# A transformer stack on one core: gate moved into the output projection's weights, residual added from PSUM, new instruction orders

## The reference

```
x = x + gate1 * (self_attention(modulate(ln(x))) @ W_o + b_o)     # gate1: one value per feature
x = x + cross_attention(ln(x) or x, context) @ W_oc + b_oc
x = x + gate2 * (gelu(modulate(ln(x)) @ W1 + b1) @ W2 + b2)
```

## Time and profile before

| | us |
|---|---|
| median of 3 runs | 2904.0 (2903.85 to 2904.89) |
| profiled execution | 2907.48 |
| its span, first to last instruction | 2905.7 |
| PE busy | 2775.7 (96%) |
| DVE busy | 1765.5 (61%) |
| ACT busy | 1542.6 (53%) |
| POOL busy | 699.1 (24%) |
| mean granted clock of PE | 0.975 |

### The profile page before, as it was taken

The page is one execution under the profiler, slowest core; times in us unless marked ns, Lnnn a source line. Parts: engine busy times, 40 slices in busy tenths (PEclk is TensorE's granted clock), DMA queues, the critical chain, the costliest instruction groups (busy, mean ns, idle before and its releaser), DMA issues. The chain is left out here.

```text
span 2905.7 us, 61884 instructions
## 1 busy us (share of the span) xinstructions
PE 2775.7 (96%) x23508; PEld 2275.6 (78%) x23508; DVE 1765.5 (61%) x3583; ACT 1542.6 (53%) x2707; POOL 699.1 (24%) x760
## 2 busy tenths in 40 slices
PE   7999999995899999999999999999999999999998
PEld 6999999994677777777777777777777777777866
DVE  2444444435576776776766767667666666666652
ACT  3444444432455555655556555655565556556653
POOL 3333343321122221222212212212122121121111
PEclk8999999996799999999999999999999999999998
DMA  5122222104335444445454443543545435445421
GB/s 160 44 78 80 69 69 69 40 8 134 95 79 114 100 104 109 102 106 124 100 143 97 101 107 95 120 105 92 130 103 136 102 90 112 99 94 109 103 66 36
DMA packets 276950, 277.90 MB, mean 96 GB/s; under 512 B 90352, under 2 KB 206432, under 8 KB 276656
## 3 DMA queue, kind: packets, MB, share of 16 engines
q1 hardware_dynamic: 264752, 251.26, 36.0%
q10 hardware_dynamic: 11904, 22.68, 2.3%
HBM read 99.03 MB, written 29.56 MB: 44 GB/s over the span
## 5 line engine op out<-in xcount | busy, mean ns | idle before, releaser
L1957 ACT ACTIVATE p_f<-score 128x1024 f32<-128x1024 f32 (+1 forms) x576 | 560.8, 1019 | 319.4 <-PE obank L3095 138.5
L2459 DVE TENSOR_REDUCE m_a<-score 128x4 f32<-128x1024 f32 x384 | 458.3, 1217 | 48.2 <-PE score L3061 48.1
L3165 PE MATMUL gbank<-w,h_c 128*128 128x256 f32 x1536 | 396.0, 392 | 1.9 <-ACT h_c L1974 1.9
L3165 PEld LDWEIGHTS gbank<-w,h_c 128*128 128x128 f32 x1536 | 274.6, 190 | 48.1 <-ACT h_c L1974 2.3
L1146 PE MATMUL m_ps<-m_comb,m_w 128*128 128x256 f32 x2304 | 295.4, 284 | 1.5 <-PEq L253 1.5
L1146 PEld LDWEIGHTS m_ps<-m_comb,m_w 128*128 128x128 f32 x2304 | 279.9, 188 | 5.0 <-issue 3.6
L819 ACT ACTIVATE m_hf<-m_ps,tab 128x256 f32<-128x256 f32 x192 | 80.5, 470 | 246.9 <-PE m_ps L1146 246.9
L1781 POOL TENSOR_TENSOR res_a<-res_a,bias_a 128x512 f32<-128x512 f32 x48 | 64.2, 1336 | 577.3 <-DMA bias_a<-rows_L 577.3
L3095 PE MATMUL obank<-p_f,v_s 128*20 128x256 f32 x3072 | 200.8, 391 | 1.1 <-ACT p_f L1957 0.8
L761 POOL TENSOR_TENSOR m_hhl<-m_hf,m_hhl 128x512 fp32r<-128x512 f32 x96 | 125.2, 1304 | 318.8 <-DVE m_hhl L985 318.8
L1789 POOL TENSOR_TENSOR c_rstd<-c_mv,eps 128x2 f32<-128x2 f32 x48 | 9.3, 194 | 742.3 <-DVE c_mv L2412 742.3
(11 more groups left out here) (282 smaller groups left out, 5572.6 us busy)
## 6 DMA issues: line engine op xcount, KB each, us to landing
k_cat<-k_hl SPq DMA_DIRECT2D x288, 128.0 KB, 3.6
q_cat<-q_hl SPq DMA_DIRECT2D x288, 128.0 KB, 4.1
qc_cat<-qc_hl SPq DMA_DIRECT2D x288, 128.0 KB, 3.2
split_L<-m_cut SPq DMA_DIRECT2D x24, 512.0 KB, 5.8
x_a<-x_after_L SPq DMA_DIRECT2D x48, 256.0 KB, 4.0
res_a<-x_after_L SPq DMA_DIRECT2D x48, 256.0 KB, 2.8
kc_cat<-kc_hl SPq DMA_DIRECT2D x288, 39.0 KB, 1.9
x_after_L<-y_c SPq DMA_DIRECT2D x32, 256.0 KB, 3.2
```

The lines of the kernel that those rows point to most:

```text
L1957: e.activation(p_f[i % 4][0:n, :], score[i % 2].ap[0:n, :, :].rearrange("p h n -> p (h n)"), ACT.Exp, scale=SCALE).then_inc(ex.sem, 1)
L2459: e.tensor_reduce(m_a[:, :, i::NPAIR].rearrange("p t h -> p h t"), score[i % 2].ap[:, :, :].rearrange("p h (t k) -> p h t k", t=TT), AX.X, ...
L3165: mm = e.matmul(B_DOWN.ap[:, tt, :], h_c[:, k, tt * P:(tt + 1) * P], weights_of(d)["w2"][:, k, :], start=(k == 0), stop=(k == MC - 1))
```

## The change

The self projection multiplies by weights whose columns already carry the gate: POOL makes them per unit (`self_out_gated`), one unit ahead. The input is loaded straight into x_b, POOL adds the bias row there, and DVE adds the projection out of PSUM. res_a is gone. The loads of the input now wait for cross_residual and cross_turned of the unit before.

```
-        x_a, res_a = tile("x_a"), tile("res_a")
+        x_a = tile("x_a")
+        o_gated = sb("o_gated", [P, CC, D])
 load_residual(a):                                            # SP
-                    e.wait_ge(*S["T_xb"].at(a - 1))
-                x_load(a, res_a, S["A_x"])
+                    e.wait_ge(*S["K_res"].at(a - 1))
+                    e.wait_ge(*S["K_xt"].at(a - 1))
+                x_load(a, x_b, S["A_x"])
 self_residual(a):                                            # POOL
-                    bias_added(res_a, res_a, bias_a[:, :], S["A_res"])
-            def self_sum(a):
-                    e.wait_ge(*S["T_y"].at(a))
-                    e.wait_ge(*S["A_res"].at(a))
-                    e.tensor_tensor(x_b[:, :, :], x_b[:, :, :], res_a[:, :, :], ALU.add).then_inc(S["T_xb"].sem, 1)
+                    bias_added(x_b, x_b, bias_a[:, :], S["A_res"])
+            def self_out_gated(a):                            # POOL
+                e.wait_ge(*S["A_gate"].at(a))
+                if a:
+                    e.wait_ge(*S["T_op"].at(a - 1))
+                if a % NB == 0:
+                    e.wait_ge(*W_in["o"].at(a // NB))
+                e.tensor_tensor(o_gated[:, :, :], W["o"][:, :, :], gate_a[:, :].unsqueeze(1).to_broadcast([P, CC, D]),
+                                ALU.mult).then_inc(S["T_og"].sem, 1)
-            def self_gated(a):                                # DVE
-                e.wait_ge(*S["A_gate"].at(a))
-                    e.wait_ge(*S["K_res"].at(a - 1))
-                    e.wait_ge(*S["K_xt"].at(a - 1))
-                e.tensor_tensor(x_b[:, :, :], B_T.ap[:, :, :], gate_a[:, :].unsqueeze(1).to_broadcast([P, TT, D]),
-                                ALU.mult).then_inc(S["T_y"].sem, 1)
+            def self_sum(a):                                  # DVE
+                e.wait_ge(*S["T_op"].at(a))
+                e.wait_ge(*S["A_res"].at(a))
+                e.tensor_tensor(x_b[:, :, :], B_T.ap[:, :, :], x_b[:, :, :], ALU.add).then_inc(S["T_xb"].sem, 1)
 self_projected(a):                                           # PE
-                weights_in(a, "o")
-                turn(B_T, S["T_y"], a)
-                by_token(B_T, 0, oT_a, W["o"])
+                e.wait_ge(*S["T_og"].at(a))
+                turn(B_T, S["T_xb"], a)
+                by_token(B_T, 0, oT_a, o_gated)
```

The written-out orders of all engines are new, in the loop as well as in the opening and the drain. PE's loop (+ the beginning of one iteration after, - before):

```
+ self_plain(m, 4); cross_values(b, 2); cross_values(b, 3); up(c, 1); self_plain(m, 5); self_plain(m, 6);
+ self_recips_spread(a); cross_keys_values(a); self_projected(a); up(c, 2); self_plain(m, 7); self_turned(q);
+ up(c, 3); self_max_rows(m); cross_turned(a); keys(q); cross_queries(a); cross_recips_spread(b); queries(q);
+ self_scores(n - 2, 0); self_scores(n - 2, 1); cross_projected(b); down(n - 5, 0..3); self_values(n - 2, 0); ...
- cross_keys_values(n - 4); self_turned(n - 2); self_max_rows(n - 3); cross_turned(n - 4); up(n - 6, 3);
- cross_queries(n - 4); keys(n - 2); queries(n - 2); self_scores(a, 0..1); cross_recips_spread(n - 5); down(d, 0..1);
- self_scores(a, 2..3); cross_projected(n - 5); down(d, 2); ... up(c, 0); up(c, 1); self_recips_spread(a);
- self_plain(m, 4..5); cross_values(b, 3); self_projected(a); context_turned(a); self_plain(m, 6..7); up(c, 2)
```

POOL's loop, before and after:

```
- context_rstd(n - 2); cross_residual(a); self_residual(n - 2); mlp_sum(n - 5); self_rstd(n); mlp_residual(n - 4);
- self_sum(n - 2); cross_rstd(n - 2); mlp_rstd(n - 3)
+ context_rstd(n - 2); mlp_rstd(n - 4); self_rstd(n); mlp_sum(n - 5); self_residual(n - 2); self_out_gated(n - 1);
+ mlp_residual(n - 4); cross_rstd(n - 2); cross_residual(n - 2)
```

```
-            e.wait_ge(*S["store"].at(NB - 1))
+            e.wait_ge(*S["store"].at(NB - 2))
+            e.wait_ge(s_last, 16)                              # DVE, blocks
+            e.memset(k_cat[0][:, :, :].bitcast(F32), -1.0).then_inc(s_ones, 1)
```

```
-            e.wait_ge(s_first, 64)
+            e.wait_ge(s_qk, 1)
+            e.tensor_copy(mix["wqk"][:, :, :], ps_qk[:, :, :]).then_inc(s_done, 1)
+            e.wait_ge(*S["xt"].at(0))
+            e.wait_ge(s_first, 48)
```

More of the change, by code:

```diff
@@ L3429, in _ @@
             self_plain(3, 4)
+            cross_values(1, 3)
             up(0, 1)
+            self_plain(3, 5)
             self_recips_spread(2)
-            self_plain(3, 5)
             self_plain(3, 6)
-            cross_values(1, 3)
+            cross_keys_values(2)
             self_projected(2)
+            up(0, 2)
             self_plain(3, 7)
-            up(0, 2)
+            self_turned(4)
+            up(0, 3)
+            self_max_rows(3)
+            cross_turned(2)
+            keys(4)
+            cross_queries(2)
+            queries(4)
+            cross_recips_spread(1)
+            self_scores(3, 0)
+            self_scores(3, 1)
+            down(0, 0)
+            down(0, 1)
+            down(0, 2)
+            cross_projected(1)
+            self_scores(3, 2)
+            self_scores(3, 3)
+            down(0, 3)
+            self_values(3, 0)
+            cross_plain(2, 0, 0)
+            cross_plain(2, 0, 1)
+            self_scores(3, 4)
+            self_values(3, 1)
+            cross_plain(2, 1, 0)
+            cross_plain(2, 1, 1)
+            down(0, 4)
+            self_scores(3, 5)
+            cross_plain(2, 2, 0)
+            self_scores(3, 6)
+            cross_plain(2, 2, 1)
+            down(0, 5)
+            cross_plain(2, 3, 0)
+            self_scores(3, 7)
+            cross_plain(2, 3, 1)
+            down(0, 6)
+            cross_max_rows(2)
+            down(0, 7)
+            self_plain(4, 0)
+            self_plain(4, 1)
+            self_values(3, 2)
+            mlp_turned(1)
+            self_values(3, 3)
+            cross_scores(2, 0)
+            cross_scores(2, 1)
+            values(4, 0)
+            values(4, 1)
+            cross_scores(2, 2)
+            cross_values(2, 0)
+            cross_values(2, 1)
+            context_turned(3)
+            cross_scores(2, 3)
+            self_plain(4, 2)
+            up(1, 0)
+            self_plain(4, 3)
             for n in range(6, 47):
@@ L3441, in _ @@
                     e.wait_ge(s_w[layer(n)], 16 * n_w[layer(n)])
-                cross_keys_values(n - 4)
-                self_turned(n - 2)
-                self_max_rows(n - 3)
-                cross_turned(n - 4)
-                up(n - 6, 3)
-                cross_queries(n - 4)
-                keys(n - 2)
-                queries(n - 2)
-                self_scores(a, 0)
-                self_scores(a, 1)
-                cross_recips_spread(n - 5)
-                down(d, 0)
-                down(d, 1)
@@ L3545, in _ @@
-            self_values(44, 3)
-            self_plain(45, 1)
-            cross_scores(43, 0)
-            mlp_turned(42)
-            values(45, 0)
-            cross_scores(43, 1)
-            cross_scores(43, 2)
-            values(45, 1)
-            context_turned(44)
-            cross_scores(43, 3)
-            cross_values(43, 0)
-            cross_values(43, 1)
+                self_turned(q)
+                up(c, 3)
+                self_max_rows(m)
+                cross_turned(a)
@@ new lines, in _ @@
+                cross_plain(n - 3, 3, 1)
+                down(n - 5, 6)
+                cross_max_rows(n - 3)
+                down(n - 5, 7)
+                self_plain(n - 1, 0)
+                self_plain(n - 1, 1)
+                self_values(n - 2, 2)
+                self_values(n - 2, 3)
+                mlp_turned(n - 4)
+                values(n - 1, 0)
+                cross_scores(n - 3, 0)
+                cross_scores(n - 3, 1)
+                values(n - 1, 1)
+                context_turned(n - 2)
@@ L3633, in _ @@
             up(43, 2)
+            cross_keys_values(45)
+            self_turned(47)
+            self_max_rows(46)
             self_projected(45)
-            self_turned(47)
             up(43, 3)
-            self_max_rows(46)
             cross_turned(45)
```

1143 lines of the change are left out of this document (550 added, 593 removed).

## The result

The kernel after takes 2891.8 us (median of 4, 2887.7 to 2895.8), the kernel before in the same session 2904.4 us. The ratio is 0.9943, 95% interval 0.9929 to 0.9958: faster by 0.57%, which is 16.5 us (the two medians lie 12.7 us apart), beyond the 0.2% that can be told from nothing. The direction was forecast, the 44 us were not: about a third of them came, and 2891.8 lies at the edge of the stated range of 2826 to 2892.

What follows compares the result with a forecast made beforehand. PE bounds the steady loop (busy 1790 of 1838 us). Terms of 16, 8, 5.3, 10, 2.4 and 2 sum to 44 us off the profiled 2907.5, giving 2863.5, or 2860 for the runs' median; range 2826 to 2892.

Steps and rivals of the forecast that it cites:

- x_a's wait less gelu's: Steady loop: 1.15 us of wait removed before cross_turned, 0.75 added before self_turned; 0.40 net per iteration, 16 us.
- The border: Before the blocks: no wait for the last store, and k_cat fills moved off self_normed(0); 5.3 us won.
- The preparation: Before the border: router rows and context copy come earlier, the gain capped by the anchor loads; 2.4 us won.
- Rival C: SyncE's load_residual waits for cross_residual and holds up the max rows: 82 us lost in the loop, 2942 us; chance 0.08.
- The other edges in the loop: Steady loop: SyncE's and ScalarE's orders, the gate's row and the residual landing in x_b cost nothing, hidden by PE's work.
- rival B: The removed wait returns whole at self_turned and cross_turned, GpSimd's chain having 0.3 us to spare: 2876 or 2884 us; chance 0.20.
- The loop: The 41 steady iterations: 16 us from the exchanged waits and 8 us from the joints.
- the joints: Steady loop: down(d, 0..3) made contiguous wins 0.2 us per iteration, 8 us.
- Filling: From 669.5 to 819.5 us: self_turned(2), values(1) and queries put in gaps win 10 us.
- Rival D: The order does as forecast, but preparation and filling give nothing: 2872 us; chance 0.12.
- The drain: Final stretch of 248.5 us: one GpSimd link less per unit wins 2 us, bounds -3 and 6.
- rival A: Steady loop: no gelu stall, or a faster chain after it, so the whole 1.15 us goes: 2829 us; chance 0.15.

Runs made afterwards that it cites:

- e3_gate_only: Kernel before with only the gate moved onto the projection's weights and the residual added from PSUM, orders otherwise kept: ratio 0.9992 to the kernel before.
- e6_normed_later: Kernel after with VectorE's self_normed(n) moved behind self_max(n-1, 0) and (n-1, 1): ratio 0.9895 to the kernel before.
- e1_border: Kernel before with only the new preparation and border; loops, filling and drain in the old orders: ratio 0.9984 to the kernel before.
- e13b_filling: Kernel after with context_stats(0) and context_normed(0) behind keys_low(0) and ScalarE's five weight loads issued first: ratio 0.9933 to the kernel before.
- e2: Kernel before with only up(c, 3) moved ahead of self_max_rows and cross_turned in the loop: ratio 1.0259, 75 us slower.
- e7: Kernel after with ScalarE's five weight loads issued at the start of the blocks: ratio 0.9945 to the kernel before.
- e8: Kernel after with VectorE's context_stats(0) and context_normed(0) moved behind keys_low(0): ratio 0.9940 to the kernel before.
- e10: Kernel of e6_normed_later with ScalarE's next_queries_keys also moved behind cross_weights(n-3, 0): ratio 0.9882 to the kernel before.
- e11: Kernel after with the sixteen matmuls of down(0..3) cut again into 8, 4 and 4: ratio 1.0013 to the kernel before.
- e12b_bank_again: Kernel after with self_turned writing bank g1 instead of g0, run again for its profile: 2895.7 us in one execution.
- e9_three: Kernel after with self_turned on g1, self_normed behind two self_max, and mlp_residual behind cross_rstd and held until xT_b is made: 2850.7 us, ratio 0.9806.
- e5_bank_pool: Kernel after with self_turned on g1 and GpSimd's cross_rstd ahead of mlp_residual: ratio 0.9961 to the kernel before.

## Why the prediction was right in direction and wrong in size

**What held.** The bound, PE's stalls of one place in the loop. The wait for x_a went. The new stall before self_turned: forecast 0.70 as idle time, "in its place 41 waits of about 0.7 us"; it is 41 of 0.59. Of the loop's terms x_a's wait less gelu's: forecast 0.40 net, measured 0.98 - 0.59 = 0.39, 16 us in 41 periods. The border: forecast 5.3; x_a's first turn is 7.5 us earlier and the mixture's last group 2.1 (645.52 against 647.65), which leaves 5.3. (By the earlier trace rows the prediction had the normalising end 0.8 us past the fills. It ends at 669.41, 1.0 us past the two of k_cat, and behind them came a third fill, of kc_cat, which ended at 668.95.) The preparation: 2.4 forecast, 2.2 measured (the mixture begins at 59.51, before at 61.69). The gate on the projection: nil, and e3_gate_only shows it. Rival C did not come: 3.5 us of waits for max rows, and their cause is the weights in ScalarE's queue, not load_residual in SyncE's.

**The failed steps.**

1. "The other edges in the loop ... I cost at nothing: PE's work hides them." The list named SyncE's and ScalarE's orders and left VectorE's out. There self_normed(n) was put between mlp_gated and self_max(n-1, 0), just when GpSimd starts mlp_sum; it takes 1.7 us, and cross_scores waits. By the periods of e6_normed_later this place costs 0.52 us, 21 us in 41: the largest miss (the timed runs show 14 of it). What makes it 1.7 us long is the collision of the earlier trace rows, which I had used for the border and for rival B, and not looked for elsewhere in the new orders.
2. The loop: 24 us forecast (16 and 8), 9.5 measured. Per period, from the runs: x_a's wait -0.98, the joints, by what is left over, -0.1 (forecast -0.2), the old order's irregular losses -0.36 (not forecast), gelu +0.59, self_max +0.52 (not forecast), and the two long periods +0.13 (5.4 us over 41, not forecast). Sum -0.20; measured -0.23. The rest of 0.03 is layer 3, whose periods are 0.11 shorter. So the two waits that the prediction weighed against each other came out at its 0.40, and the loop missed by terms that it did not have. The 0.13 is of one execution: in others each of these two periods loses between nothing and 4.3 us.
3. "Filling ... I take 10", and with it "Preparation" and "The border" as terms that simply add. 17.7 us were to stand at the fifth turn, and 0 stand there. No row priced the filling, and its new order put two waits in: the context's stats ahead of the first cast, and 2.5 MB of weights, the first of them ahead of the first max rows. Rival D had preparation and filling at nothing but kept the border; in fact the border's gain was lost too. e1_border shows that the gains of preparation and border exist (the fifth turn 8.4 us earlier under the old filling), and e13b_filling that most of them come back without the two waits. The 10 us of the filling itself exist in no run: from the first turn to the fifth the new order takes 7.6 us longer than the old, and 2.5 longer without the two waits.
4. The drain: 2 forecast, bounds to 6; 5.7 measured, by luck in part. From the last of these turns to the end the old drain takes 245.5 to 248.1 us in four profiles (before, e1, e2, e3), the new one 242.4 to 246.5 in seven (after, e6, e7, e8, e10, e11, e13b), and after is the shortest of them; the means are 3 us apart. No run took it apart.

**Rival B** did not come: its sign, a wait on xn_b, is absent in after. What it said of the chain was nearly right. The projection's chain had not 0.3 us to spare but none (e12b_bank_again), and yet it added no wait in after, since the stall for gelu ahead of it left just the time that the chain takes. So rival A's premise, that the stall alone could go and give all its time, was excluded, as the prediction said ("the stall alone going would not win its full 0.75"); it took an edit of the chain too (e9_three).

What stays open: what in the old order made periods vary by up to 1.4 us (the waits of PE there, x_a apart, come to 5 us of the 15), how much of the 0.52 us is the collision and how much the mere place of self_normed, and why the new filling, freed of its two waits, is still longer than the old.

## What to carry to other kernels

Of a reordered schedule, check every engine's list, and for each pair of VectorE and GpSimd instructions ask what will run beside them: here a standstill of 1 us on a VectorE instruction that PE does not read next stood ahead of PE's second largest stall. A stall removed in a balanced loop can uncover the next chain at once, so edits that give nothing at first (the bank alone, the bank with GpSimd's order) can give 24 us once what stands behind them is mended as well (e6_normed_later to e9_three), and one that helps in its setting can cost 75 us outside it. Bulk loads are better issued behind the small rows that are urgent, and an early gain must be followed to the first point where the streams meet before it is put into a sum.

## What the runs showed of the hardware

- The same 128x256 normalising of VectorE takes 0.40 us alone. When a 128x512 instruction of GpSimd runs beside it, it ends some 0.15 us after GpSimd's end, which makes it 1.37 us for x_a in after and 1.33 in the mean for xn_b in e5_bank_pool; beside GpSimd's three fills in a row it took 4.17 (kernel before, 664.93). Reductions from PSUM beside GpSimd's self_residual in after (1606.67, two in 2.34 us) take their usual 1.2 us.
- From the end of a VectorE instruction to the start of PE's that waits for it some 0.15 to 0.2 us pass (x_a's first turn in after: 661.93 to 662.08), so two rows 0.18 us apart are no slack.
- Cutting a run of sixteen matmuls twice cost 0.53 us, 0.26 per cut (e11_downs_split).
- A wait of 1.64 us on PE at full clock was followed by ten us at a mean granted clock of 0.59 and 0.73; one of 1.8 us later was followed by no fall.
- With ScalarE's five transfers of 512 KB issued from 695.08 us on, SyncE's 16 KB rows, issued at 695.47, reached PE 5 us after it wanted them; with the five issued first, 0.9 us.
